# Stacking the bfloat16 parts of Q and K through DRAM instead of SBUF to SBUF, in a one-core decoder layer

## Chip, cores and metric

One core of one Trainium2 chip. The metric is the device time of one execution in microseconds. Engines: TensorE (PE, with PEld for its weight loads), VectorE (DVE), ScalarE (ACT), GpSimd (POOL) and SyncE (SP), which issues nearly all DMAs.

## What is computed

One pre-norm decoder layer on x of 4 x 256 x 256 (float32):

```
x = x + attn(layernorm(x))              # 16 heads of 16, rotary q and k, causal softmax, Wout
x = x + adjacency(ctx, layernorm(x))    # sim = Q K^T of ctx; keep the top 76 of 256 per row,
                                        # sigmoid, symmetrise: (1-g)*layernorm(x) + g*A
x = x + moe(layernorm(x))               # 64 experts of width 96, 6 of them per token,
                                        # grouped top-k routing, and a shared expert
```

## The kernel before, in words

The work has two phases. The attention phase goes over the four batches b = 0 to 3 (256 tokens each). Its steps run in one hand-written order for all engines, the list STEPS (line 73): every engine walks through the list and runs its own function for a step, if it has one (the `run` dictionaries, lines 686, 830, 987, 1387). The entries F4, F31 and so on in the list are VectorE's filler: so many instructions of the top-k search of the adjacency (maximum of 8 and match-replace, lines 1053 and 1058). The MoE phase follows: routing on VectorE, then 32 pairs of experts, with weights streamed through a ring of 16 slots and tokens gathered and scattered by GpSimd's indirect DMAs.

Q and K must keep float32 precision in the score product but go through TensorE as bfloat16. So each is split in three bfloat16 parts (part 0 the cast, part 1 the cast of the rest, part 2 what is left), and six of the products of parts are stacked along the contraction: for each head, Q's stack `qst` has 6 groups of 16 partitions that hold parts 0, 0, 0, 1, 1, 2 (TERMS_Q, line 59), K's stack `kst` has parts 0, 1, 2, 0, 1, 0. One matmul over 96 partitions then gives all six products.

The steps around the change, for one b:

- A2a (line 1127): VectorE reads the projected q and k out of PSUM, shuffles them and multiplies by the cosine; A2b adds the sine part (VectorE for b = 0, GpSimd after, lines 1143 and 930); ScalarE's `first_part` (757) casts to part 0.
- A2c, A2d: `first_rest` (VectorE 1150 or GpSimd 936), ScalarE's `second_part` (763), `third_part` (1155 or 941). GpSimd's third_part is followed by `gamma_constants` at b = 1 (902, its last instruction clears the tile `zero`) and by `moe_constants` at b = 2 (913).
- The parts stand in `parts` (184), one of two buffers by b % 2; the second buffer lies in slots 2 to 7 of `ring_dn`, the ring of expert down-weights. A part is 128 partitions of 1024 elements (Q has 2 x 256 of them, K the rest); partition p = 8 d + g holds dimension d of head pair g.
- SP's `stack` (359), in step A2d: for each part it waits until the part is there, then copies it with one DMA per place in the stacks, SBUF to SBUF. 12 DMAs of 128 KB for each b; a destination is 16 partitions of 8 KB. For b = 3 SP first waits for the last units of b = 0, whose stack it overwrites (373). After the stacks of b = 3 SP clears the scattered expert rows in DRAM with eight DMAs of 768 KB out of `zero` (380).
- U0 to U5 (521): TensorE computes six "S units" of scores of batch b (lines 478, 479) and six "T units" (490, 491) of batch b - 1. U0 waits for the whole stack of b (526). VectorE takes the maxima of each S unit (1176) and frees its bank, ScalarE exponentiates each T unit (784), GpSimd masks it (963), TensorE multiplies with the values (502, 506).
- V0 (`routing_constants`, 967): GpSimd fills constants of the MoE phase, among them the 32 unused partitions of `ring_dn` (973), a memset of 32 x 4096. It waits for the stacks of b = 3, since the second buffer of the parts lies there.
- D3a (1218, 1094): VectorE normalises the MoE's input, TensorE transposes it (577).

A wait on every DMA is by a semaphore that counts 16 for each. SP issues in order and waits in order.

Of the kernel before, what the change touches and what calls it, by code (L numbers as in the profile page):

```python
# [15 lines left out]
P = 128  # L16
# [18 lines left out]
RA = 8  # L35
# [79 lines left out]


def decoder_kernel(nc, x, cosT, sinT, ctxT, wxT, wqkvT, woT, gamma, gate_w, bias, w_gu, w_dn, ws_gu, ws_dn, out):
    x3_dram = nc.dram_tensor("moe_input", [T, E], F32, kind="Internal").ap()
    z_dram = nc.dram_tensor("expert_rows", [T * 8, E], F32, kind="Internal").ap()

    with ExitStack() as ctx:
# [40 lines left out]
        def cut(phase, *shape, dt=F32):  # L162
# [7 lines left out]
            if len(shape) > 1:  # L170
# [10 lines left out]
        xnT = cut(AT, 2, 2, S)  # L181
        qkc = cut(AT, 4, S)
        qks = cut(AT, 4, S)
        parts = [cut(AT, 3, 4, S, dt=BF16),
                 ring_dn[:, RA - 6:].rearrange("p r e n -> p (r e n)")[:, 0:6 * S].bitcast(BF16).rearrange("p (j a s) -> p j a s", j=3, a=4)]

        qst1, kst1 = cut(AT, H, S, dt=BF16), cut(AT, H, S, dt=BF16)
        simS = cut(AT, NT, S)
# [78 lines left out]

        x_in = [sem(f"x_in{b}") for b in range(B)]
        ctx_in, gamma_in, rope_in, wqkv_in, wo_in, moe_in = (sem(n) for n in ("ctx_in", "gamma_in", "rope_in", "wqkv_in", "wo_in", "moe_in"))
        stack_in = [sem(f"stack_in{b}") for b in range(B)]  # L270
        x3_out = sem("x3_out")
        z_zeroed = sem("z_zeroed")
# [65 lines left out]
        def _(sp):  # L338
# [17 lines left out]
                sp.dma_start(gate_up_weights(p).rearrange("p e c n -> p (e c n)"), w_gu[p]).then_inc(ring_in[p % RP], 16)  # L356
                sp.dma_start(down_weights(p)[0:FF].rearrange("p e n -> p (e n)"), w_dn[p]).then_inc(ring_in[p % RP], 16)

            def stack(b, j):

                sp.wait_ge((part0, part1, part2)[j], b + 1)
                for a, dst, terms in ((0, qst, TERMS_Q), (1, kst, TERMS_K)):
                    src = parts[b % 2][:, j, 2 * a:2 * a + 2, :].rearrange("p c s -> p (c s)")
                    for n, term in enumerate(terms):
                        if term == j:
                            to = dst[b % 3][n * D:(n + 1) * D].rearrange("p (g c) s -> p g (c s)", c=2)
                            sp.dma_start(to, src).then_inc(stack_in[b], 16)

            later = {("A2d", 1): range(0, 1), ("A2d", 2): range(1, RA - 6), ("D3a", 1): range(RA - 6, RA), ("D3a", 3): range(RA, RP)}
            for stage, b in STEPS:  # L370
                if stage == "A2d":
                    if b >= 3:
                        filled(sp, "unit", (T_UNITS[-1], b - 3))
                    for j in range(3):
                        stack(b, j)
                    if b == B - 1:
                        sp.wait_ge(zero_ready, 1)
                        zv = z_dram.rearrange("(t p k) n -> t p k n", p=P, k=8)
                        for t in range(NT):
                            sp.dma_start(zv[t, :, 0:KE, :], zero[:, :].unsqueeze(1).broadcast_to((P, KE, E))).then_inc(z_zeroed, 16)  # L380
                if stage == "D3a":
                    sp.wait_ge(x3_ready, b + 1)
                    sp.dma_start(x3_dram.rearrange("(t p) e -> p t e", p=P)[:, TPB * b:TPB * b + TPB, :],
                                 x3[:, TPB * b:TPB * b + TPB, :]).then_inc(x3_out, 16)
                if (stage, b) == ("D3a", 1):
                    filled(sp, "unit", (T_UNITS[-1], 2))
                if (stage, b) == ("D3a", B - 1):
                    filled(sp, "gen", ("att", B - 1))
                for p in later.get((stage, b), ()):
                    ring_fill(p)  # L390
# [24 lines left out]
        def _(pe):  # L415
# [105 lines left out]
            def units(n):  # L521
                def step(b):
                    if n == 0 and b >= 1:
                        emptied(pe, "gen", ("mT", b - 1))
                    if n == 0 and b < B:
                        pe.wait_ge(stack_in[b], 16 * 2 * len(TERMS_Q))
                    if b >= 1:
                        t_unit(b - 1, T_UNITS[n])
                    if b < B:
                        s_unit(b, S_UNITS[n])  # L530
                    if b >= 1 and n >= 3:
                        pv(b - 1, n - 3)
                return step
# [188 lines left out]
        def _(sc):  # L722
# [33 lines left out]

            def first_part(b):
                sc.wait_ge(roped, b + 1)
                if b >= 2:
                    sc.wait_ge(stack_in[b - 2], 16 * 2 * len(TERMS_Q))  # L760
                nc.scalar.copy(parts[b % 2][:, 0], qkc).then_inc(part0, 1)

            def second_part(b):
                sc.wait_ge(rest_ready, b + 1)
                nc.scalar.copy(parts[b % 2][:, 1], qkc).then_inc(part1, 1)

            def head_outputs(b, half):
                filled(sc, "out", (half, b))
# [90 lines left out]
        def _(gp):  # L859
# [53 lines left out]
            def moe_constants():  # L913

                link(pool.memset(tri[:, :], 1.0))
                link(pool.affine_select(out=tri[:, :], in_=tri[:, :], compare_op=ALU.is_ge, fill=0.0, base=-1,
                                        pattern=[[1, P]], channel_multiplier=-1))
                link(pool.memset(ones[:, :], 1.0))
                link(pool.iota(iotac[:, :, :], pattern=[[1, CAP], [0, NT]], base=-CP, channel_multiplier=0, allow_small_or_imprecise_dtypes=True))
                link(pool.memset(keep[:, :, :], 1.0))  # L920
                pool.memset(keep[:, :, 0:1], 0.0).then_inc(order_ready, 1)
                gp.wait_ge(order_ready, 1)

            def times_sin(b):
# [11 lines left out]
            def first_rest(b):  # L936
                if b >= 1:
                    gp.wait_ge(part0, b + 1)
                    pool.tensor_tensor(qkc, qkc, parts[b % 2][:, 0], ALU.subtract).then_inc(rest_ready, 1)

            def third_part(b):
                if b >= 1:
                    gp.wait_ge(part1, b + 1)
                    pool.tensor_tensor(parts[b % 2][:, 2], qkc, parts[b % 2][:, 1], ALU.subtract).then_inc(part2, 1)
                if b == 1:
                    gamma_constants()
                if b == 2:
                    moe_constants()
# [18 lines left out]
            def routing_constants(_):  # L967

                filled(gp, "gen", ("v", B - 1))
                gp.wait_ge(stack_in[B - 1], 16 * 2 * len(TERMS_Q))  # L970
                filled(gp, "unit", (T_UNITS[-1], 1))
                link(pool.memset(gsum, NEG))
                link(pool.memset(ring_dn[FF:P].rearrange("p a e n -> p (a e n)"), 0.0))
                link(pool.memset(gpick, NEG))
                link(pool.memset(epick, 3 * NEG))
                link(pool.memset(cand[:, :, NE:], 3 * NEG))
# [47 lines left out]
        def _(ve):  # L1024
# [125 lines left out]
            def first_rest(b):  # L1150
                if b == 0:
                    ve.wait_ge(part0, 1)
                    v.tensor_tensor(qkc, qkc, parts[b % 2][:, 0], ALU.subtract).then_inc(rest_ready, 1)

            def third_part(b):
                if b == 0:
                    ve.wait_ge(part1, 1)
                    v.tensor_tensor(parts[b % 2][:, 2], qkc, parts[b % 2][:, 1], ALU.subtract).then_inc(part2, 1)

            def shifts_turned(b):  # L1160
                if b >= 1:
# [59 lines left out]
            def routing(n):  # L1221
# [3 lines left out]
                ts = slice(t0, t1)  # L1225
                gs = slice(t0 * NG, t1 * NG)
                if n == 0:
                    ve.wait_ge(stack_in[B - 1], 16 * 2 * len(TERMS_Q))
                    filled(ve, "gen", ("v", B - 1))
                    ve.wait_ge(pick_ready, 1)  # L1230
                ve.wait_ge(score_ready, n + 1)
# [273 lines left out]
```

## Time and profile before

| | |
|---|---|
| median of 3 runs | 388.62 us (387.64 to 391.87) |
| profiled execution, its own time | 388.62 us |
| its span in the trace | 386.8 us |
| mean granted TensorE clock | 0.754 |
| busy: PE, PEld, DVE, ACT, POOL | 265.6, 192.3, 249.5, 90.3, 156.3 us |
| chain that ended last | PE 40%, DVE 25%, issue 8%, POOL 4%, DMA 2%, ACT 1% |
| stack DMAs | 48 of 128 KB |

The profiled execution's own time is the median itself; 1.8 us of it lie outside the span. The page gives busy times of each engine and the span in 40 slices of 9.67 us; the trace answers by line, by time (timeline), by stretch (windows) and by the chain of waits.

### The profile page before, as it was taken

To read this page: it belongs to the slowest core of one execution; us is meant where nothing else is said; L and a number is where in the kernel's file an instruction comes from. 1 tells how busy PE (TensorE), PEld (TensorE's weight loads), DVE (VectorE), ACT (ScalarE), POOL (GpSimd) and SP (SyncE) were. 2 spreads that over 40 slices of the span, in tenths; PEclk is the share of its full clock that TensorE was granted. 3 is DMA by queue.
4 is the path that set the end of the run, shared out by engine and by line. 5 is a ranking of instruction groups with operands and counts; after the bars stand their busy time and mean duration, and the time that the engine had idled before them with its cause. 6 is when DMAs were issued, how large, how long until landed. Compare 5 with 4: busy or idle time off the path is not lost.

```text
span 386.8 us, 6223 instructions
## 1 busy us (share of the span) xinstructions
PE 265.6 (69%) x2293; PEld 192.3 (50%) x2293; DVE 249.5 (64%) x655; ACT 90.3 (23%) x166; POOL 156.3 (40%) x160
## 2 busy tenths in 40 slices
PE   4681673686887895884915979998987979694000
PEld 1461653573674783653404468766656665362000
DVE  3769999996597558967699973241513403242897
ACT  2056001424332232441403000021211212241000
POOL 3727804848114123248833034225626244554000
PEclk9897767597997598797665776567857667999555
DMA  6349940950899300850009902146748460102982
GB/s 194 121 67 120 124 78 9 127 91 2 101 227 386 132 2 1 248 148 27 0 14 271 233 15 68 39 140 177 230 141 234 133 182 31 51 33 73 359 275 79
DMA packets 32141, 48.18 MB, mean 125 GB/s; under 512 B 4644, under 2 KB 22534, under 8 KB 32112
## 3 DMA queue, kind: packets, MB, share of 16 engines
q1 hardware_dynamic: 29424, 42.90, 45.2%
q0 software_dynamic: 2688, 4.89, 4.6%
q8 instruction: 18, 0.29, 0.3%
q14 instruction: 11, 0.09, 0.1%
HBM read 31.36 MB, written 12.58 MB: 114 GB/s over the span
## 4 chain that ended last, share of the span: by engine, by line
PE 40%; DVE 25%; issue 8%; POOL 4%; DMA 2%; ACT 1%; another core or an unknown queue 0%; POOLq 0%; DVEq 0%; SPq 0%
PE unit L667 8%; PE gen L644 7%; DVE arena L1453 6%; PE proj L682 4%; PE gen L635 3%; PE gen L569 2%; PE outp L675 2%; DVE arena L1058 2%; PE unit L490 2%; PE unit L653 2%; PE unit L491 2%; PE unit L478 2%; DVE arena L1176 1%; POOL expert_rows L1010 1%; PE unit L595 1%
## 5 line engine op out<-in xcount | busy, mean ns | idle before, releaser
L1010 POOL DMA_INDIRECT expert_rows<-arena x32 | 32.0, 1002 | 50.5 <-ACT arena L853 44.5
L1435 DVE TENSOR_TENSOR arena<-arena,unit 128x96 f32<-128x96 f32 x32 | 8.1, 252 | 60.9 <-ACT arena L846 57.0
L1005 POOL DMA_INDIRECT arena<-moe_input,arena x24 | 27.2, 1133 | 37.8 <-DVE arena L1372 31.4
L1176 DVE TENSOR_REDUCE arena<-unit 128x4 f32<-128x1024 f32 (+1 forms) x24 | 29.0, 1214 | 13.9 <-PE unit L479 13.9
L644 PE MATMUL gen<-arena 128*48 128x8 bf16 x512 | 28.2, 231 | 10.8 <-issue 10.1
L963 POOL TENSOR_SCALAR_AFFINE_SELECT arena<-arena 128x512 f32<-128x512 f32 (+1 forms) x24 | 19.2, 804 | 40.6 <-ACT arena L784 40.6
L784 ACT ACTIVATE arena<-unit 128x1024 f32<-128x1024 f32 x24 | 24.6, 1024 | 37.2 <-PE unit L491 37.2
L644 PEld LDWEIGHTS gen<-arena 128*48 128x48 bf16 x512 | 26.6, 184 | 11.9 <-issue 10.9
L1053 DVE MAX8 arena<-arena 128x8 f32<-128x256 f32 x80 | 29.9, 413 | 0.6 <-ACT arena L741 0.4
L1058 DVE MATCH_REPLACE8 arena<-arena 128x256 f32<-128x256 f32 x72 | 28.9, 408 | 0.0
L491 PE MATMUL unit<-arena 128*128 128x256 bf16 (+1 forms) x128 | 28.5, 281 | 0.0
L478 PE MATMUL unit<-arena 96*128 96x128 bf16 (+1 forms) x96 | 20.0, 292 | 8.8 <-DMA arena<-arena 7.9
L1453 DVE TENSOR_REDUCE arena<-arena 128x256 f32<-128x1536 f32 (+1 forms) x9 | 22.0, 2446 | 4.4 <-DMA arena<-expert_rows 4.4
L479 PE MATMUL unit<-arena,identb 128*128 128x128 bf16 x128 | 24.6, 253 | 0.0
L490 PE MATMUL unit<-arena 96*128 96x128 bf16 (+1 forms) x96 | 21.2, 279 | 3.9 <-ACT arena L784 3.9
L667 PE MATMUL unit<-ring,arena 128*64 128x192 f32 x128 | 18.8, 428 | 0.0
L880 POOL TENSOR_SCALAR srs<-mv 128x2 f32<-128x2 f32 x12 | 3.6, 299 | 36.2 <-DVE mv L1087 36.2
L853 ACT ACTIVATE arena<-proj,arena 128x256 f32<-128x256 f32 x32 | 15.2, 474 | 12.8 <-PE proj L682 10.2
L667 PE MATMUL unit<-arena 128*64 128x192 f32 x128 | 17.6, 407 | 0.5 <-issue 0.5
L460 PE MATMUL proj<-arena 128*128 128x256 f32 x64 | 16.6, 417 | 1.4 <-ACT arena L747 1.4
L478 PEld LDWEIGHTS unit<-arena 96*128 96x128 bf16 x96 | 11.6, 121 | 11.0 <-issue 8.2
L846 ACT ACTIVATE arena<-unit 128x96 f32<-128x96 f32 x32 | 8.0, 251 | 37.6 <-PE unit L667 37.6
(191 smaller groups left out, 616.2 us busy)
## 6 DMA issues: line engine op xcount, KB each, us to landing
ring<-in_w_gu SPq DMA_DIRECT2D x16, 384.0 KB, 6.6
expert_rows<-zero SPq DMA_DIRECT2D x8, 768.0 KB, 10.0
arena<-in_w_gu SPq DMA_DIRECT2D x16, 384.0 KB, 3.4
arena<-expert_rows SPq DMA_DIRECT2D x7, 768.0 KB, 5.8
arena<-ring_dn SPq DMA_DIRECT2D x24, 128.0 KB, 7.0
ring_dn<-in_w_dn SPq DMA_DIRECT2D x16, 192.0 KB, 6.9
arena<-in_w_dn SPq DMA_DIRECT2D x16, 192.0 KB, 4.0
arena<-arena SPq DMA_DIRECT2D x12, 128.0 KB, 5.9
```

Source lines behind the costliest of these rows:

```text
L478: mm(area, qst[b % 3][0:KT, h, t * P:(t + 1) * P], kst[b % 3][0:KT, h, 0:n], start=True, stop=False)
L479: last = mm(area[:, n - P:n], identb[:, :], masks, start=False, stop=True)
L490: mm(area, kst[b % 3][0:KT, h, kt * P:(kt + 1) * P], qst[b % 3][0:KT, h, kt * P:S], start=True, stop=False)
L491: last = mm(area, sel[:, h, :], nmT[:, kt * P:S], start=False, stop=True)
L644: last = mm(gen[CP * e:CP * e + CAP, q * 8:(q + 1) * 8], hotbuf[:, g % 2, 2 * q + e, :, t], vals[:, t, EPG * g + 2 * q + e, :], start=(t = ...
L667: last = mm(unit[CP * e:CP * e + CP, 1, (p % 2) * 512:(p % 2) * 512 + 2 * FF], xgT[:, g % 2, c, first:first + CP], gate_up_weights(p)[:, e ...
L1005: pool.indirect_dma_start(out=xg[:, k % NX, :], out_offset=None, in_=x3_dram, in_offset=bass.IndirectOffsetOnAxis(ap=toki[:, k:k + 1], axi ...
L1010: pool.indirect_dma_start(out=z_dram, out_offset=bass.IndirectOffsetOnAxis(ap=rowi[:, p:p + 1], axis=0), in_=yrow[:, p % NY, :], in_offset ...
L1053: last[i] = mark(v.max(best[:, i, :], simS[:, t + i, :] if r == 0 else work[:, i, :]))
L1058: last[i] = mark(v.match_replace(work[:, i, :], best[:, i, :], simS[:, t + i, :] if r == 0 else work[:, i, :], NEG))
L1176: v.tensor_reduce(nmax[:, t, c * u:c * u + c], unit_at((key, b)).rearrange("p (h k) -> p h k", k=n), axis=AX, op=ALU.max, negate=True).the ...
L1453: link(v.reduce_sum(fin[:, i % NZ, cols], zin[:, i % NZ, :, cols].rearrange("p k e -> p e k"), axis=AX))
```

## The change

The parts go through a new DRAM tensor `qk_dram`. For each b SP stores each part with one DMA of 256 KB (`store`), and loads the stacks from there with six DMAs (`load`): runs of neighbouring groups of 16 partitions go as one DMA where their parts are the same (Q's 0, 0, 0 and 1, 1: the source is repeated by a stride of zero) or follow each other (K's 0, 1, 2 and 0, 1). SP waits for each store before the loads that read it. There is one buffer of parts now: ScalarE's first_part of b waits for the three stores of b - 1. The clearing of the expert rows moves from behind the stacks of b = 3 to behind those of b = 1. The memset of ring_dn moves from GpSimd's routing_constants to the end of its moe_constants. Waits on the stacks of b = 3 that protected the parts become waits on its stores.

```diff
--- before.py
+++ after.py
@@ -115,6 +115,7 @@
 
 
 def decoder_kernel(nc, x, cosT, sinT, ctxT, wxT, wqkvT, woT, gamma, gate_w, bias, w_gu, w_dn, ws_gu, ws_dn, out):
+    qk_dram = nc.dram_tensor("qk_parts", [B, 2, 3, P, TPB * S], BF16, kind="Internal").ap()
     x3_dram = nc.dram_tensor("moe_input", [T, E], F32, kind="Internal").ap()
     z_dram = nc.dram_tensor("expert_rows", [T * 8, E], F32, kind="Internal").ap()
 
@@ -181,8 +182,7 @@
         xnT = cut(AT, 2, 2, S)
         qkc = cut(AT, 4, S)
         qks = cut(AT, 4, S)
-        parts = [cut(AT, 3, 4, S, dt=BF16),
-                 ring_dn[:, RA - 6:].rearrange("p r e n -> p (r e n)")[:, 0:6 * S].bitcast(BF16).rearrange("p (j a s) -> p j a s", j=3, a=4)]
+        parts = cut(AT, 3, 4, S, dt=BF16)
 
         qst1, kst1 = cut(AT, H, S, dt=BF16), cut(AT, H, S, dt=BF16)
         simS = cut(AT, NT, S)
@@ -267,6 +267,7 @@
 
         x_in = [sem(f"x_in{b}") for b in range(B)]
         ctx_in, gamma_in, rope_in, wqkv_in, wo_in, moe_in = (sem(n) for n in ("ctx_in", "gamma_in", "rope_in", "wqkv_in", "wo_in", "moe_in"))
+        parts_out = [[sem(f"parts_out{b}_{j}") for j in range(3)] for b in range(B)]
         stack_in = [sem(f"stack_in{b}") for b in range(B)]
         x3_out = sem("x3_out")
         z_zeroed = sem("z_zeroed")
@@ -356,24 +357,39 @@
                 sp.dma_start(gate_up_weights(p).rearrange("p e c n -> p (e c n)"), w_gu[p]).then_inc(ring_in[p % RP], 16)
                 sp.dma_start(down_weights(p)[0:FF].rearrange("p e n -> p (e n)"), w_dn[p]).then_inc(ring_in[p % RP], 16)
 
-            def stack(b, j):
+            def store(b, j):
 
                 sp.wait_ge((part0, part1, part2)[j], b + 1)
+                sp.dma_start(qk_dram[b, :, j].rearrange("a p n -> p a n"), parts[:, j].rearrange("p (a c) s -> p a (c s)", a=2)).then_inc(parts_out[b][j], 16)
+
+            def load(b, newest):
+
+
+                sp.wait_ge(parts_out[b][newest], 16)
                 for a, dst, terms in ((0, qst, TERMS_Q), (1, kst, TERMS_K)):
-                    src = parts[b % 2][:, j, 2 * a:2 * a + 2, :].rearrange("p c s -> p (c s)")
-                    for n, term in enumerate(terms):
-                        if term == j:
-                            to = dst[b % 3][n * D:(n + 1) * D].rearrange("p (g c) s -> p g (c s)", c=2)
-                            sp.dma_start(to, src).then_inc(stack_in[b], 16)
+                    for n, m in ((0, 3), (3, 2), (5, 1)):
+                        if max(terms[n:n + m]) != newest:
+                            continue
+                        to = dst[b % 3][n * D:(n + m) * D].rearrange("p h s -> p (h s)")
+                        src = qk_dram[b, a].rearrange("j (d h) n -> (j d) (h n)", d=D)
+                        if m > 1 and terms[n] == terms[n + 1]:
+                            src = src[terms[n] * D:(terms[n] + 1) * D].unsqueeze(0).broadcast_to((m, D, H * S))
+                        else:
+                            src = src[terms[n] * D:(terms[n] + m) * D]
+                        sp.dma_start(to, src).then_inc(stack_in[b], 16)
 
             later = {("A2d", 1): range(0, 1), ("A2d", 2): range(1, RA - 6), ("D3a", 1): range(RA - 6, RA), ("D3a", 3): range(RA, RP)}
             for stage, b in STEPS:
                 if stage == "A2d":
                     if b >= 3:
                         filled(sp, "unit", (T_UNITS[-1], b - 3))
-                    for j in range(3):
-                        stack(b, j)
-                    if b == B - 1:
+                    store(b, 0)
+                    store(b, 1)
+                    load(b, 0)
+                    store(b, 2)
+                    load(b, 1)
+                    load(b, 2)
+                    if b == 1:
                         sp.wait_ge(zero_ready, 1)
                         zv = z_dram.rearrange("(t p k) n -> t p k n", p=P, k=8)
                         for t in range(NT):
@@ -523,7 +539,7 @@
                     if n == 0 and b >= 1:
                         emptied(pe, "gen", ("mT", b - 1))
                     if n == 0 and b < B:
-                        pe.wait_ge(stack_in[b], 16 * 2 * len(TERMS_Q))
+                        pe.wait_ge(stack_in[b], 16 * 6)
                     if b >= 1:
                         t_unit(b - 1, T_UNITS[n])
                     if b < B:
@@ -756,13 +772,14 @@
 
             def first_part(b):
                 sc.wait_ge(roped, b + 1)
-                if b >= 2:
-                    sc.wait_ge(stack_in[b - 2], 16 * 2 * len(TERMS_Q))
-                nc.scalar.copy(parts[b % 2][:, 0], qkc).then_inc(part0, 1)
+                if b >= 1:
+                    for j in range(3):
+                        sc.wait_ge(parts_out[b - 1][j], 16)
+                nc.scalar.copy(parts[:, 0], qkc).then_inc(part0, 1)
 
             def second_part(b):
                 sc.wait_ge(rest_ready, b + 1)
-                nc.scalar.copy(parts[b % 2][:, 1], qkc).then_inc(part1, 1)
+                nc.scalar.copy(parts[:, 1], qkc).then_inc(part1, 1)
 
             def head_outputs(b, half):
                 filled(sc, "out", (half, b))
@@ -918,7 +935,8 @@
                 link(pool.memset(ones[:, :], 1.0))
                 link(pool.iota(iotac[:, :, :], pattern=[[1, CAP], [0, NT]], base=-CP, channel_multiplier=0, allow_small_or_imprecise_dtypes=True))
                 link(pool.memset(keep[:, :, :], 1.0))
-                pool.memset(keep[:, :, 0:1], 0.0).then_inc(order_ready, 1)
+                link(pool.memset(keep[:, :, 0:1], 0.0))
+                pool.memset(ring_dn[FF:P].rearrange("p a e n -> p (a e n)"), 0.0).then_inc(order_ready, 1)
                 gp.wait_ge(order_ready, 1)
 
             def times_sin(b):
@@ -936,12 +954,12 @@
             def first_rest(b):
                 if b >= 1:
                     gp.wait_ge(part0, b + 1)
-                    pool.tensor_tensor(qkc, qkc, parts[b % 2][:, 0], ALU.subtract).then_inc(rest_ready, 1)
+                    pool.tensor_tensor(qkc, qkc, parts[:, 0], ALU.subtract).then_inc(rest_ready, 1)
 
             def third_part(b):
                 if b >= 1:
                     gp.wait_ge(part1, b + 1)
-                    pool.tensor_tensor(parts[b % 2][:, 2], qkc, parts[b % 2][:, 1], ALU.subtract).then_inc(part2, 1)
+                    pool.tensor_tensor(parts[:, 2], qkc, parts[:, 1], ALU.subtract).then_inc(part2, 1)
                 if b == 1:
                     gamma_constants()
                 if b == 2:
@@ -967,10 +985,10 @@
             def routing_constants(_):
 
                 filled(gp, "gen", ("v", B - 1))
-                gp.wait_ge(stack_in[B - 1], 16 * 2 * len(TERMS_Q))
+                for j in range(3):
+                    gp.wait_ge(parts_out[B - 1][j], 16)
                 filled(gp, "unit", (T_UNITS[-1], 1))
                 link(pool.memset(gsum, NEG))
-                link(pool.memset(ring_dn[FF:P].rearrange("p a e n -> p (a e n)"), 0.0))
                 link(pool.memset(gpick, NEG))
                 link(pool.memset(epick, 3 * NEG))
                 link(pool.memset(cand[:, :, NE:], 3 * NEG))
@@ -1150,12 +1168,12 @@
             def first_rest(b):
                 if b == 0:
                     ve.wait_ge(part0, 1)
-                    v.tensor_tensor(qkc, qkc, parts[b % 2][:, 0], ALU.subtract).then_inc(rest_ready, 1)
+                    v.tensor_tensor(qkc, qkc, parts[:, 0], ALU.subtract).then_inc(rest_ready, 1)
 
             def third_part(b):
                 if b == 0:
                     ve.wait_ge(part1, 1)
-                    v.tensor_tensor(parts[b % 2][:, 2], qkc, parts[b % 2][:, 1], ALU.subtract).then_inc(part2, 1)
+                    v.tensor_tensor(parts[:, 2], qkc, parts[:, 1], ALU.subtract).then_inc(part2, 1)
 
             def shifts_turned(b):
                 if b >= 1:
@@ -1225,7 +1243,8 @@
                 ts = slice(t0, t1)
                 gs = slice(t0 * NG, t1 * NG)
                 if n == 0:
-                    ve.wait_ge(stack_in[B - 1], 16 * 2 * len(TERMS_Q))
+                    for j in range(3):
+                        ve.wait_ge(parts_out[B - 1][j], 16)
                     filled(ve, "gen", ("v", B - 1))
                     ve.wait_ge(pick_ready, 1)
                 ve.wait_ge(score_ready, n + 1)
```

## Rows read from the trace of the kernel before

**Rows 1.** The page, busy tenths of VectorE in 40 slices.

```profile
DVE  3769999996597558967699973241513403242897
```

**Rows 2.** The chain that ended last, first 135 us: start, us, what.

```profile
75.03 0.74 DVE arena L1053 x2
...
82.69 1.29 DVE arena L1133
...
89.35 1.04 ACT ring_dn L761
...
101.92 0.16 PE unit L490
```

**Rows 3.** Timeline of all engines, 18 to 72 us: start, us, engine, line.

```profile
24.37 1.04 ACT L765 CAST arena<-arena 128x1024 bf16<-128x1024 f32 x1 [0.80 <-DVE arena L1153]
...
25.45 1.23 DVE L1158 TENSOR_TENSOR arena<-arena 128x1024 bf16<-128x1024 f32 x1 [1.11 <-ACT arena L765]
...
33.60 1.04 ACT L761 CAST ring_dn<-arena 128x1024 bf16<-128x1024 f32 x1 [0.73 <-POOL arena L934]
...
38.65 0.27 PE L478 MATMUL unit<-arena 96*128 96x128 bf16 x1 [7.85 <-DMA arena<-arena]
...
42.01 2.55 PE L467 MATMUL gen<-arena 128*128 128x256 f32 x8
...
42.73 2.34 DVE L1176 TENSOR_REDUCE arena<-unit 128x8 f32<-128x1024 f32 x2
```

**Rows 4.** Timeline of VectorE: the normalisation of the MoE input, b = 2 and b = 3.

```profile
176.50 4.12 DVE L1094 TENSOR_SCALAR x<-res,mv,rstd 128x256 f32<-128x256 f32 x2 [0.57 <-POOL rstd L881]
...
201.03 0.73 DVE L1094 TENSOR_SCALAR x<-res,mv,rstd 128x256 f32<-128x256 f32 x2 [0.51 <-POOL rstd L881]
```

**Rows 5.** The chain that ended last, 165 to 232 us.

```profile
176.54 3.69 issue
...
180.77 1.10 PE gen L577 x4
```

**Rows 6.** Timeline of GpSimd.

```profile
78.67 0.64 POOL L963 TENSOR_SCALAR_AFFINE_SELECT arena<-arena 128x512 f32<-128x512 f32 x1 [0.93 <-ACT arena L784]
84.05 2.35 POOL L928 TENSOR_TENSOR arena<-arena 128x1024 f32<-128x1024 f32 x1 [4.75 <-DVE arena L1133]
...
176.65 3.51 POOL L973 MEMSET ring_dn<- 32x4096 f32 x1
...
181.47 3.52 POOL L979 MEMSET arena<- 128x4096 bf16 x1
```

**Rows 7.** Timeline of TensorE: its first product with the values.

```profile
87.04 0.64 PE L502 MATMUL outp<-arena 128*32 128x256 f32 x8
```

**Rows 8.** Timeline of SP's DMA issues.

```profile
23.10 7.76 SPq L367 DMA_DIRECT2D arena<-arena  x12
...
66.07 9.57 SPq L367 DMA_DIRECT2D ring<-arena  x12
...
105.55 16.78 SPq L380 DMA_DIRECT2D expert_rows<-zero  x8
```

**Rows 9.** Windows: us; busy of PE, PEld, DVE, ACT, POOL; clock; DMA share; GB/s.

```profile
5.00:7.00 2.00, 2.00 (x3) 0.80 (x3) 0.97 (x4) 0.00 (x0) 0.34 (x2) 1.00 1.00 391
...
212.00:214.00 2.00, 2.00 (x7) 1.55 (x6) 1.93 (x3) 1.13 (x1) 0.00 (x0) 0.50 1.07 270
...
30.00:35.00 5.00, 0.79 (x4) 0.36 (x2) 4.85 (x20) 3.92 (x5) 3.77 (x3) 0.80 1.14 123
...
118.00:123.00 5.00, 2.48 (x31) 1.63 (x30) 4.21 (x9) 1.95 (x3) 1.91 (x5) 0.87 1.09 386
```

**Rows 10.** The page, DMA issues: count, KB each, median us from issue to landing.

```profile
arena<-in_w_gu SPq DMA_DIRECT2D x16, 384.0 KB, 3.4
...
moe_input<-x SPq DMA_DIRECT2D x4, 256.0 KB, 2.2
```

## The prediction

> **What bounds the kernel now.** I read the page's slices first, then the chain of waits, then the timeline around each place that the diff touches. In the slices VectorE is busy for nine tenths and more from the fourth to the ninth, 29 to 87 us [rows 1]: this is the stretch in which the stacks of b = 0, 1 and 2 are made. The chain is followed back from the end only as far as 75 us, and there it stands on VectorE's filler, goes over the rotary step of b = 3 to ScalarE's cast of its part 0, and from 91 us on mostly over TensorE [rows 2]. Ahead of 75 us I take VectorE as the bound, since it has work without a gap from 30 us. So a thing that comes earlier between 30 and 83 us gains nothing unless VectorE waits for it, and a thing that makes VectorE wait costs in full.
>
> The one visible stall on the stacks is TensorE's: it starts the first score unit at 38.65 us after 7.85 us of waiting for the DMA [rows 3]. It looks like the target of such a change, but VectorE does not feel it. Its maxima of the first two units are taken at 42.73 us, in one run of 2.34 us, straight behind filler. The two units take TensorE from 38.65 to 42.01 us, 1.68 us each, so the first is complete at about 40.5 and the second at 42.2.
>
> A second stall is smaller in the page than on the chain: the normalisation of the MoE input of b = 2 takes 4.12 us for two instructions, where the same pair takes 0.73 us for b = 3 [rows 4]. The chain shows 3.69 us of it as "issue" and TensorE's transpose straight behind [rows 5]. What stands beside it is GpSimd's memset of ring_dn, 176.65 to 180.16 us [rows 6]: VectorE moves again when it ends.
>
> **The memset that moves.** It leaves the place where it blocks the chain. What is late next there are GpSimd's four short memsets (1.3 us, from 180.16 to 181.47) and then another of 3.52 us, which stands at 181.47 us and will follow at about 177.9 [rows 6]. VectorE's pair, started at 176.50, should be through by 177.3 to 177.6, between them. Gain: 4.12 - 0.73 = 3.4 at most, less up to 0.6 for the short ones; I take **3.1 us**. The bounds are 3.4, and 0 where the next long memset catches the pair. The rest of the chain follows it (transpose, router, shared expert, the next residual), and GpSimd's own constants come 3.5 us earlier too, so nothing there becomes late.
>
> At its new place, behind moe_constants at 76.5 us, the same 3.51 us are put ahead of two masks. The second ends at 79.3 now and would end at about 82.0; GpSimd then idles until 84.05 as before, for it had 4.75 us of idle [rows 6]. The first product with the values, which needs these masks, starts only at 87.04 us [rows 7]. VectorE's work in those microseconds is filler and a maximum out of PSUM, and it shows the same durations beside GpSimd's work earlier. Cost 0, with 2 us of cover; 2 us at most without it.
>
> **The stacks of b = 0.** Before, SP issues the 12 DMAs from 23.10 us and the stack has landed at 38.65: 15.55 us for 1.57 MB [rows 3, 8]. While they run the engines carry 123 GB/s, with every one of them busy, and the clearing of the expert rows gets 386 [rows 9]. So the stack copies are slow by their shape. Now: part 0 is stored at 23.1 and landed at 25.3 (a store of 256 KB takes 2.2 us to land [rows 10]); part 1 is there at 25.41 and part 2 at 26.68 [rows 3]. SP is held by part 1 before it issues the first loads, so these leave at about 26.1, 3.0 us later than the first copies did. The bytes loaded are the same 1.57 MB into the same partitions. By the nearest row, the copies of before, they take the same 15.55 us, and the store of part 2 among them 0.7 us (262 KB at 386). That is 26.1 + 15.55 + 0.7 = 42.3 us for the landed stack, 3.7 later than now. The store of part 2 and the last two loads are in series behind it, but in this reading the engines are full all the time, so the hops are hidden.
>
> From below: at the rates of plain loads, 270 to 391 GB/s [rows 9], part 2 would be landed at about 30.5, the last two loads issued by 31.7 and landed after 3.4 us more [rows 10], at about 35. From above: the two loads of Q whose source is repeated may not be spread evenly over the 16 engines (the second rival); that gives 47 us.
>
> What VectorE feels of a stack that lands at T: the second unit is complete at T + 3.6 and is wanted at 42.73 + 1.17 = 43.9, so the delay is T - 40.3 where positive. With T = 42.3 it is **2.0 us**, with 35 nothing, with 47 6.8. This delay goes to the end, because VectorE is full from there to the rotary step of b = 3 [rows 1, 2].
>
> A rule of the Trainium skill bears on the 123 GB/s. "SBUF — State Buffer", section "Door 1: The DMA port swizzle", says that a DMA's rate goes with how many of 16 ports its partitions reach, and 16 neighbouring partitions reach 4 of them; the page's 27 GB/s a port would give 109 here, near the 123 measured. By this rule loads of 32 or 48 partitions would run at twice the copies' rate, the stack would land near 37 us, and the term would be 0 instead of 2.0.
>
> **The stacks of b = 1 to 3, and the new waits.** ScalarE's first_part of b now waits for the stores of b - 1, with ScalarE's exponentials and copies queued behind it. For b = 1 the cast stands at 33.60 [rows 3] and the stores of b = 0 are in by 31 to 36: up to 2 us, which VectorE does not wait for. For b = 3 it stands on the chain at 89.35 [rows 2]. The stores of b = 2 come behind the clearing, which has moved. SP is done with b = 1 at about 53, then holds 16.8 us in the eight clearing DMAs [rows 8], so b = 2 starts at about 70 instead of 66.07, behind some 6 us of queued bytes. The store of part 2 lands at about 84, 5 us ahead of the cast, which by then is 2 us later too. The stack of b = 2 is wanted at 101.92 [rows 2] and lands near 90; b = 1 and b = 3 have more room. The clearing itself leaves 105 to 129 us, where nobody on the chain waits for a DMA. All this: 0, the bound above being the third place of the second rival.
>
> **The sum**, against the profiled execution's 388.6, which is also the median: 388.6 - 3.1 + 2.0 = **387.5 us**.
>
> **Rivals.** *First: the loads run well, and only the memset counts.* For it: plain loads reach 270 to 391 GB/s [rows 9]. Against it: they write the rows that took 123. The time is 388.6 - 3.1 = 385.5.
>
> *Second, slower than before: the repeated source puts two loads on few DMA engines.* The outermost dimension of the source is the 3 or the 2 repetitions. If a DMA is dealt out by that dimension, 128 KB of each of the two loads go through one engine, and all that is behind them in its queue waits, the store of part 2 first. One engine carries 391 / 16 = 24 GB/s at best and 270 / 16 = 17 in a stretch of weight loads [rows 9]: 5.4 to 7.7 us for 128 KB, twice, in series. T = 26.7 + twice that + 3.5 to 4.9 for the other shares of this engine and the landing = 41.0 to 47.0; VectorE's delay is 0.7 to 6.7 us. The midpoint, 3.7, with the memset's gain gives 389.2, the far end 392.2. It is slower than before where T is past 43.4. At the far end the store of part 2 of b = 2 also nears the cast at 89.35. For it: the copies show that the shape alone can cost a factor of three. Against it: no DMA of the trace has so small an outer dimension, so it can't be seen. The Trainium skill states it outright: "DMA: Bandwidth & Descriptors", section "Rules for kernel authors", says that a leading zero-stride broadcast of c copies confines the whole DMA to at most c engines; no row here shows it.
>
> *Third: the long memset behind catches the normalisation.* The gain of 3.1 goes, and with the stacks' 2.0 it is 390.6. Against it: VectorE got in between two memsets at 180.2 us, where the gap is equally short [rows 5, 6].
>
> *That the stall of 7.85 us was worth something* I give no case of its own: it would need VectorE to be idle ahead of 42.73, and it is not.
>
> **How the numbers follow.** 387.5: 0.38. First rival 0.27, second 0.22, third 0.08, others 0.05. The likeliest one's own range is 386 to 389. One per cent, 3.9 us, is about what can be told from no change here. Faster by over that, below 384.7, needs the first rival and another microsecond of gain, for which small shifts between VectorE and GpSimd are enough: 0.18. Slower than 392.5 needs the second at its far end with a wait of ScalarE on top: 0.12. Between them 0.70. The range of 8 in 10 is 384.4 to 392.0.
>
> **What would show it.** In the changed profile the normalisation of b = 2 takes under 1.3 us and no "issue" of over 1 us stands before the transpose; the memset stands at about 77 us (plus the delay) with GpSimd still idle behind it. TensorE's first score unit starts at 41 to 44 us, and VectorE shows a wait of some 2 us in front of the first maxima. A start at 35 and no wait says the first rival; the repeated loads landing 3 us or more after their neighbours say the second. A wait of ScalarE at line 761 of b = 3 would make the prediction wrong from the other side, as would a normalisation that is still at 4 us.

## The result, and the profile after

The changed kernel takes 390.48 us (median of 20, 386.97 to 394.32) where the kernel before takes 386.06 beside it (20, 383.43 to 392.27): a ratio of 1.0099, 95% interval 1.0069 to 1.0129, which is 3.8 us slower. Ratios in this document are taken over fast executions, those that did not run slow as a whole, so the medians of all executions differ by a little more, 4.4 us. The forecast was 1.1 us faster. Each profile is of one execution, and from about 226 us on the changed one ran without TensorE's "issue" gaps that the others have: 0.3 us idle ahead of the experts' products (L660) against 10.8 before. Its span is 367.2 us; the same kernel's next profile, the run again below, has 382.8. So profiles are compared below by stage, never by their ends.

First the page of the changed kernel, where its chain stood by engine and by line:

```profile
PE 44%; DVE 22%; DMA 15%; SPq 7%; issue 5%; POOL 3%; ACT 3%; POOLq 0%; ACTq 0%; DVEq 0%
DMA qk_parts<-arena 12%; PE unit L683 7%; PE gen L660 7%; DVE arena L1472 6%; SPq L396 4%; PE proj L698 4%; PE gen L651 3%; PE unit L611 2%; PE proj L639 2%; PE gen L585 2%; PE proj L449 2%; POOL expert_rows L1028 2%; PE outp L691 2%; PE unit L669 2%; DVE arena L1076 2%
```

The DMA had 2% of the chain before. Now it has 15%, 12% in stores of parts, and SP's own queue has 7%. The chain itself (start, us, what) says where, and it answers to [rows 2]:

```profile
26.21 0.86 SPq L379
27.55 11.01 DMA qk_parts<-arena
38.66 1.05 ACT arena L778
39.73 7.86 DMA qk_parts<-arena
47.60 0.72 SPq L379
48.84 9.64 DMA qk_parts<-arena
60.38 4.04 SPq L396
...
79.28 5.84 DMA qk_parts<-arena
85.14 0.71 SPq L379
86.38 10.58 DMA qk_parts<-arena
97.05 1.04 ACT arena L778
```

Read it as a sentence: a store of part 2 that lands after 11 us (a store of 256 KB took 2.2 us before [rows 10]) holds ScalarE's cast of b = 1; SP, held in the loads of b = 1, comes late to the clearing (L396), which holds the stores of b = 2; these hold the cast of b = 3. That cast stands at 97.05, 7.7 us behind the 89.35 of [rows 2]. Now SP's timeline, then TensorE's and VectorE's at the first score units, against [rows 3, 8]:

```profile
23.46 2.71 SPq L363 DMA_DIRECT2D qk_parts<-arena  x2
26.21 1.29 SPq L379 DMA_DIRECT2D arena<-qk_parts  x2
27.55 0.41 SPq L363 DMA_DIRECT2D qk_parts<-arena  x1
28.01 1.14 SPq L379 DMA_DIRECT2D arena<-qk_parts  x2
...
38.57 0.78 SPq L379 DMA_DIRECT2D arena<-qk_parts  x2
```

```profile
46.99 0.27 PE L494 MATMUL unit<-arena 96*128 96x128 bf16 x1 [15.84 <-DMA arena<-qk_parts]
...
48.89 1.22 DVE L1194 TENSOR_REDUCE arena<-unit 128x8 f32<-128x1024 f32 x1 [5.72 <-PE unit L495]
50.60 1.23 DVE L1194 TENSOR_REDUCE arena<-unit 128x8 f32<-128x1024 f32 x1 [0.48 <-PE unit L495]
```

SP issues four of the six loads by 29.2 us. The last two come 9.4 us later, since they need part 2 and its store, queued behind the first repeated load, lands only at 38.56. The stack of b = 0 lands at 47.0, and VectorE, which had no gap here before, waits 6.2 us. The windows say why (us; busy of five engines; clock; DMA share; GB/s):

```profile
32.00:34.00 2.00, 0.00 (x0) 0.00 (x0) 2.00 (x9) 1.23 (x2) 1.92 (x1) 0.88 0.20 61
34.00:36.00 2.00, 0.00 (x0) 0.00 (x0) 2.00 (x11) 0.00 (x0) 0.00 (x0) 0.50 0.20 61
36.00:38.00 2.00, 0.00 (x0) 0.00 (x0) 2.00 (x8) 0.00 (x0) 0.00 (x0) 0.50 0.18 60
...
45.00:46.00 1.00, 0.00 (x0) 0.00 (x0) 0.00 (x0) 0.00 (x0) 0.73 (x4) 0.50 0.07 29
46.00:47.00 1.00, 0.01 (x1) 0.04 (x2) 0.00 (x0) 0.00 (x0) 1.00 (x1) 0.50 0.06 22
```

A busy share of 0.18 to 0.20 is 3 of 16 engines, at 61 / 3 = 20 GB/s each; the copies of before kept all of them busy [rows 9]. If the load with three repetitions of 128 KB runs on three engines, it takes, by estimate, 131 KB / 20 GB/s = 6.5 us. In the last 2 us before the stack lands the share is 0.07 and 0.06, one engine of 16, which had more queued than the rest. The profile does not tell which load that engine carried. The Trainium skill's "DMA: Bandwidth & Descriptors", section "Rules for kernel authors", says that a source with a leading zero-stride dimension of c copies confines the DMA to at most c engines. The trace agrees for the load of three copies, with the share of 3 engines from 32 to 38 us; it does not show the load of two by itself.

ScalarE's timeline has the two casts that wait for a store, of b = 1 and b = 3:

```profile
38.66 1.05 ACT L778 CAST arena<-arena 128x1024 bf16<-128x1024 f32 x1 [5.42 <-DMA qk_parts<-arena]
...
97.05 1.04 ACT L778 CAST arena<-arena 128x1024 bf16<-128x1024 f32 x1 [5.69 <-DMA qk_parts<-arena]
```

Last the memset: GpSimd's timeline and VectorE's normalisation of b = 2, against [rows 4, 6]:

```profile
83.67 3.51 POOL L939 MEMSET ring_dn<- 32x4096 f32 x1
...
91.10 2.35 POOL L946 TENSOR_TENSOR arena<-arena 128x1024 f32<-128x1024 f32 x1 [2.17 <-DVE arena L1151]
...
181.49 3.51 POOL L997 MEMSET arena<- 128x4096 bf16 x1
```

```profile
180.09 0.76 DVE L1112 TENSOR_SCALAR x<-res,mv,rstd 128x256 f32<-128x256 f32 x2 [0.56 <-POOL rstd L898]
```

The pair takes 0.76 us instead of 4.12 and is done before the next long memset begins; at its new place the memset leaves GpSimd idle behind its masks, as forecast. The Trainium skill's "SBUF — State Buffer", section "Who interferes with whom", says that a VectorE instruction in a mode that uses both of its port pairs, which tensor_scalar can enter, shares one pair with GpSimd, and that the second to issue is blocked for the whole instruction of the first. The 4.12 us that end with a 3.51 us memset, and the 0.76 without it, agree; which mode the instruction ran in the trace does not show.

### The profile page after: what moved, and what is told of

It is laid out like the page before. It is cut to its first block, busy times and chain, and to the rows that moved or that the text cites. A ratio compares the mean times of both kernels' runs of the same rounds, so it can differ in the third digit from the quotient of the medians.

```text
span 367.2 us, 6217 instructions
## 1 busy us (share of the span) xinstructions
PE 253.0 (69%) x2293; PEld 184.1 (50%) x2293; DVE 244.7 (67%) x655; ACT 90.6 (25%) x166; POOL 155.7 (42%) x160
## 4 chain that ended last, share of the span: by engine, by line
PE 44%; DVE 22%; DMA 15%; SPq 7%; issue 5%; POOL 3%; ACT 3%; POOLq 0%; ACTq 0%; DVEq 0%
DMA qk_parts<-arena 12%; PE unit L683 7%; PE gen L660 7%; DVE arena L1472 6%; SPq L396 4%; PE proj L698 4%; PE gen L651 3%; PE unit L611 2%; PE proj L639 2%; PE gen L585 2%; PE proj L449 2%; POOL expert_rows L1028 2%; PE outp L691 2%; PE unit L669 2%; DVE arena L1076 2%
## 5 line engine op out<-in xcount | busy, mean ns | idle before, releaser
L494 PE MATMUL unit<-arena 96*128 96x128 bf16 (+1 forms) x96 | 18.9, 281 | 17.4 <-DMA arena<-qk_parts 15.8
L507 PE MATMUL unit<-arena 128*128 128x256 bf16 (+1 forms) x128 | 27.1, 271 | 0.0
L660 PE MATMUL gen<-arena 128*48 128x8 bf16 x512 | 24.4, 232 | 0.3 <-ACT arena L838 0.3
L506 PE MATMUL unit<-arena 96*128 96x128 bf16 (+1 forms) x96 | 21.3, 280 | 4.6 <-ACT arena L801 4.6
L660 PEld LDWEIGHTS gen<-arena 128*48 128x48 bf16 x512 | 23.7, 186 | 0.4 <-ACT arena L838 0.3
L495 PE MATMUL unit<-arena,identb 128*128 128x128 bf16 x128 | 23.2, 243 | 0.0
L683 PE MATMUL unit<-arena 128*64 128x192 f32 x128 | 16.6, 388 | 0.0
```

Source lines behind the costliest of these rows:

```text
L494: mm(area, qst[b % 3][0:KT, h, t * P:(t + 1) * P], kst[b % 3][0:KT, h, 0:n], start=True, stop=False)
L495: last = mm(area[:, n - P:n], identb[:, :], masks, start=False, stop=True)
L507: last = mm(area, sel[:, h, :], nmT[:, kt * P:S], start=False, stop=True)
L660: last = mm(gen[CP * e:CP * e + CAP, q * 8:(q + 1) * 8], hotbuf[:, g % 2, 2 * q + e, :, t], vals[:, t, EPG * g + 2 * q + e, :], start=(t = ...
L683: last = mm(unit[CP * e:CP * e + CP, 1, (p % 2) * 512:(p % 2) * 512 + 2 * FF], xgT[:, g % 2, c, first:first + CP], gate_up_weights(p)[:, e ...
```

## Experiments

All were timed in turn with the kernel before, in three batches, each on one chip (a ratio is to the kernel before on the same chip): again, split, memset_back and clear_back; split_memset_back, split_clear_back, memset_only and two_buffers; the repeats and split_b0.

**again**: the changed kernel itself.

> The changed kernel once more, to have a second profile of it beside its time. Few-engines theory (each load of Q with a repeated source runs on as many DMA engines as there are repetitions, and what stands behind it in their queues is late): ratio to before 1.01; TensorE's first score unit at 47 us, VectorE waits about 6 us for it, ScalarE's cast of part 0 of b = 3 waits 5 to 6 us for a store. The MoE phase, 142 us in the first profile of the changed kernel against 160 before, has the same instructions in both; if the difference belongs to the execution and not to the change, it comes out elsewhere here.

389.35 us, ratio 1.0134 (1.0089 to 1.018). Slower again. In its profile the first unit starts at 46.22 us and the cast of b = 3 waits 7.72 us for a store, more than the 5 to 6 expected. The span is 382.8 us, so the short last phase of the first profile belonged to that execution.

**split**: the repeated loads as one DMA of 16 partitions for each repetition, so 9 loads for a b.

```diff
-src = src[...].unsqueeze(0).broadcast_to((m, D, H * S))
+for i in range(m):
+    sp.dma_start(to[i * D:(i + 1) * D], src[...]).then_inc(stack_in[b], 16)
...
-pe.wait_ge(stack_in[b], 16 * 6)
+pe.wait_ge(stack_in[b], 16 * 9)
```

> The changed kernel, with the repeated loads issued as one plain DMA of 16 partitions for each repetition (nine loads for each b instead of six, the same bytes). Few-engines theory: the first score unit starts at 35 to 39 us, VectorE's wait of 6 us and both long waits of ScalarE go, and what is left of the change is the memset's gain: ratio to before about 0.991. Slow-rows theory (the loads are slow because of the partitions they write, as the SBUF copies of before were): the first unit stays at 42 us or later and the ratio above 1.0. Two-hops theory (the way through DRAM is what costs): the store of part 2 still lands 8 us or more after its issue.

377.85 us, ratio 0.9813 (0.9766 to 0.9859): 0.032 or some 12 us below again, beside it on the same chip, and well under the kernel before. The 0.991 expected allowed only 3.4 us for the memset; the surplus is followed up below. Its rows: TensorE's first unit, ScalarE's cast of b = 3, and a window of the loads.

```profile
39.48 0.27 PE L495 MATMUL unit<-arena 96*128 96x128 bf16 x1 [8.54 <-DMA arena<-qk_parts]
```

```profile
89.46 1.04 ACT L779 CAST arena<-arena 128x1024 bf16<-128x1024 f32 x1 [5.03 <-POOL arena L953]
```

```profile
34.00:36.00 2.00, 0.00 (x0) 0.00 (x0) 2.00 (x9) 0.78 (x1) 1.15 (x1) 0.50 1.01 172
```

All engines busy, the stack at 39.5, no wait on a store: 89.46 is within 0.1 us of [rows 2]. Issuing each repetition as a DMA of its own takes away the whole of the slow path.

**memset_back** (of the changed kernel) and **split_memset_back** (of split): the memset of ring_dn in routing_constants again.

```diff
-pool.memset(ring_dn[FF:P]...).then_inc(order_ready, 1)
...
+link(pool.memset(ring_dn[FF:P]..., 0.0))
```

> The changed kernel, with the memset of ring_dn back in GpSimd's routing constants. If VectorE's normalisation of b = 2 is blocked by that memset: it takes 4.1 us again instead of 0.76, and the kernel is 3.4 us slower than the changed one: ratio to before 1.019. If the memset costs nothing there: ratio as the changed kernel, 1.010.

> The path through DRAM with one DMA for each repetition (9 loads for a b) and the memset of ring_dn in its old place on GpSimd: the path alone, without the memset's move. Theory A, the loads on few DMA engines were the whole fault of the change and the memset's move is worth its 3.4 us: split measured 0.981, so this stands at 0.990 to 0.993 and the normalisation of b = 2 takes about 4 us again; what is left under 1 belongs to the path itself or to the earlier clearing. Rival B, the memset's new place is what made split good beyond 3.4 us: this stands at 1.00.

> The kernel of split_memset_back once more, the path through DRAM with evenly spread loads alone. It measured 1.006 where the milestones of split up to 176 us say 1.000. Theory A, no cost of the path: 0.998 to 1.004. Rival B, a cost of its own: 1.006 or more again.

memset_back: 393.76 us, 1.0246 (1.0203 to 1.0288), 4.4 us above again and above the 1.019 expected. split_memset_back: 1.006 (1.0032 to 1.0089), outside both theories and nearer rival B, and repeated 1.0015 (0.9981 to 1.0049), within theory A of the repeat. The path through DRAM with evenly spread loads alone is thus worth nothing, or costs half a per cent; it is no gain. The first run taken alone would have looked like its rival's cost.

**memset_only**: the kernel before, with only the memset moved. The second buffer of parts goes from ring_dn to x3T, so that the memset may run early, and ScalarE's first copy into x3T waits for the stacks of b = 3.

```diff
-ring_dn[:, RA - 6:]...[:, 0:6 * S].bitcast(BF16)...
+x3T.rearrange("p c t -> p (c t)")[:, 0:6 * S].bitcast(BF16)...
```

> The kernel before, with its stack copies from SBUF to SBUF, and only the memset of ring_dn moved to the end of moe_constants; so that this is free of races the second buffer of parts lies in x3T, and ScalarE's first copy into x3T waits for the stacks of b = 3, long done. Theory A: the normalisation of b = 2 falls from 4.1 to 0.7 us and the time by 3.1 to 3.4 us, 0.991 to 0.992. Rival B, the 3.4 us are taken up by a later wait in the MoE phase: 1.00.

> The kernel of memset_only once more (copies from SBUF to SBUF, the memset of ring_dn moved). Theory A: 0.983 to 0.989, the 3.4 us of the blocked normalisation and about 2 us more, since TensorE does not idle ahead of the shared expert's products of b = 3 and keeps its clock there. Rival B, only the 3.4 us: 0.991.

0.9874 (0.9834 to 0.9914), repeated 0.9848 (0.9795 to 0.9901): 4.9 and 5.9 us gained, more than the 3.4 of the blocked pair and than the 0.991 first expected. **split2**, beside the second, measured 0.9826 (0.9779 to 0.9873):

> The kernel of split once more, to see whether its 0.981 repeats on the chip on which memset_only is timed beside it. In split's profile every milestone up to 176 us stands within 0.2 us of before's (cast of b = 3 at 89.46 against 89.35, first copy of the MoE input at 127.72 against 127.63), so theory A says that the path through DRAM is worth nothing with evenly spread loads, and the memset's move all: split2 and memset_only2 agree within 1%, both at 0.982 to 0.990. Rival B, the path itself is a gain: split2 stays at 0.981 and memset_only2 above 0.987.

The two agree within their intervals, as theory A had it, so no gain of the path is seen beside that of the memset. Where the surplus over 3.4 us lies is seen between ScalarE's copies of the MoE input of b = 1 and b = 3. This takes 46.1 to 46.6 us in all four profiles with the memset in its old place (before: 156.45 to 203.04), and 40.1 to 41.0 in nine of the ten without (split: 156.53 to 197.36; split_b0, below, has 42.5). Chain pieces of memset_back, then of clear_back (below), which differs by the memset and the clearing:

```profile
182.68 3.69 issue
...
188.72 1.95 PE gen L603 x8
...
192.13 5.50 PE unit L611 x8
```

```profile
185.94 1.09 PE gen L603 x8
...
188.48 4.42 PE unit L611 x8
```

Behind the stall of 3.69 us the router's and the shared expert's products take 1.9 us more. Windows of the 6 us from the first of these transposes, in the kernel before and in clear_back, have the granted clock (third number from the right):

```profile
180.77:186.77 6.00, 4.92 (x18) 3.79 (x19) 0.81 (x2) 2.72 (x5) 5.81 (x4) 0.50 0.13 44
```

```profile
184.59:190.59 6.00, 4.92 (x19) 3.11 (x20) 2.02 (x6) 4.02 (x6) 5.87 (x3) 0.72 0.13 44
```

It is 0.50, the lower of TensorE's two levels (1.2 GHz of 2.4), for all 6 us in each of the four profiles with the stall, and 0.63 to 1.00 in the ten without. The transposes take 1.09 us in the four and 0.63 in the ten. The stall is not the only thing that the lower clock follows: split_b0 has no stall there, 0.63, and products nearly as slow.

**clear_back** (of the changed kernel) and **split_clear_back** (of split): the clearing behind the stacks of b = 3 again (`if b == 1:` to `if b == B - 1:`).

> The changed kernel, with the clearing of the expert rows back behind the stacks of b = 3. If the clearing is what makes the stores of b = 2 late: ScalarE's cast of part 0 of b = 3 waits under 1 us instead of 5.7, and the kernel is some 5 us faster than the changed one, ratio to before 0.997. If the loads of Q alone make them late: the wait stays above 4 us and the ratio at 1.01. The 6 us at the first unit of b = 0 stay in either case.

> The split loads with the memset moved, and the clearing of the expert rows in its old place behind the stacks of b = 3. With the loads of the change that edit gained some 4 us, since the clearing held up the store of b = 2. Theory A, the earlier clearing costs only where the stores are late: with the split loads nothing is waited for, so putting it back changes nothing, 0.981. Rival B, the clearing taken out of 105 to 129 us is itself where split's surplus over the memset's 3.4 us comes from: 0.990 to 0.993.

clear_back: 1.0018 (0.9982 to 1.0055), 0.0116 or some 4 us below again, a little less than expected. split_clear_back: 0.9917 (0.9887 to 0.9947), not the 0.981 of theory A but within its rival B. Memset_only, which also clears late, has 0.9874 beside it and a gain over 3.4 us, so the surplus does not need the early clearing. Split was not timed on this chip, and whether early clearing is worth something with fast loads stays open. With slow loads it costs. The cast of b = 3 in clear_back:

```profile
96.64 1.04 ACT L778 CAST arena<-arena 128x1024 bf16<-128x1024 f32 x1 [5.04 <-POOL arena L952]
```

It waits for GpSimd's half of the rotary step again, not for a store. The profile shows 1.3 us of the 4 (the table below); the rest stays open.

**two_buffers**: the changed kernel with a second buffer of parts in x3T; first_part waits for the stores of b - 2.

```diff
-parts = cut(AT, 3, 4, S, dt=BF16)
+parts = [cut(AT, 3, 4, S, dt=BF16), x3T...[:, 0:6 * S].bitcast(BF16)...]
...
-if b >= 1: ... sc.wait_ge(parts_out[b - 1][j], 16)
+if b >= 2: ... sc.wait_ge(parts_out[b - 2][j], 16)
```

> The changed kernel with its slow loads, and two buffers of parts again (the second in x3T), so that ScalarE's first_part waits for the stores of b - 2 only. Theory A, two waits make the loss, VectorE's of 6 us at b = 0 and ScalarE's of 5 to 8 us ahead of the cast of b = 3: the second one goes, and the time falls by about 4 us from that of again, 1.0134, to 1.002 to 1.005. Rival B, ScalarE's wait is hidden behind VectorE's filler and the wait at b = 0 is all: 1.013. In both the first score unit of b = 0 still starts at about 47 us.

1.0108 (1.0069 to 1.0147): a miss for theory A. ScalarE waits for no store any more, but the time barely moves; by the timed runs rival B is nearer. The table below has 0.7 and 2.7 us for that wait, not 4. Yet clear_back, in which ScalarE's wait is gone too, measured 1.0018 on another chip, and nothing in the table accounts for the difference.

**split_b0**: split's loads for b = 0 only.

> The changed kernel with the repeated loads split for b = 0 only; b = 1 to 3 keep the loads with the repeated source. Theory A, the wait of VectorE on the first stack and that of ScalarE ahead of the cast of b = 1 are 5 to 7 of the 8 us that the slow loads cost: the first unit starts at 39.5 us, the cast of b = 1 has no wait, the cast of b = 3 has a wait on the stores of b = 2 of at most 3 us beyond its usual one, and the ratio is 0.985 to 0.995. Rival B, the stacks of b = 1 to 3 cost as much: 1.00 or more.

0.9924 (0.9887 to 0.9961), within theory A. The first unit starts at 38.49 us, the cast of b = 1 waits for no store, and that of b = 3 waits for a store:

```profile
93.26 1.04 ACT L782 CAST arena<-arena 128x1024 bf16<-128x1024 f32 x1 [6.09 <-DMA qk_parts<-arena]
```

## Why the prediction was wrong

The time moved the other way than forecast. The table takes the path of the slow loads out of the profiles. The stretch runs from VectorE's shuffle of b = 1 to the cast of b = 3, 61.96 us in the kernel before (27.39 to 89.35). The ScalarE column is what the step from the cast of b = 2 to that of b = 3 has beyond 24.36 us, its length wherever no store is waited for.

| profile | VectorE's wait at the first maxima | ScalarE, cast of b = 3 | stretch beyond 61.96 |
|---|---|---|---|
| split | 0 | 0 | 0.0 |
| changed | 6.2 | 0.7 | 7.4 |
| again | 5.6 | 2.7 | 8.3 |
| clear_back | 6.9 | 0 | 7.0 |
| two_buffers | 3.3 | 0 | 3.4 |
| split_b0 | 0 | 1.1 | 1.2 |

The two waits add up to the delay within half a microsecond. Two_buffers has less of the first for a reason of its own: its projection of b = 1 took 6.10 us instead of 3.72, so VectorE came 2.3 us later to the same late stack.

- **The step that failed: the stack of b = 0.** The prediction took "the nearest row, the copies of before" for all six loads and got T = 42.3 and 2.0 us. What happened was its second rival: T = 47.0, as its bound from above said, and 6.2 us of wait against 6.7. That the landing agrees to the tenth is partly luck. The rival had 15.4 us for two loads at 17 GB/s an engine and 4.9 behind them; an engine carried 20, which makes 13 us, and the last two loads, issued at 38.57 behind the store, landed 8.4 us later. The premise, a source with only 3 or 2 outer repetitions, was in the diff. The prediction counted against it that no DMA of the trace has that shape, but this only meant that the trace could not speak on it; "the nearest row" was of another shape.
- **The second step that failed: the waits of ScalarE at b = 3, costed at 0.** The store of part 2 of b = 2 was put at 84 us, landed. It landed at 96.96: SP, held in the slow loads of b = 0 and 1, came to the clearing at 59.33 us instead of 53 and to the stores of b = 2 at 79.28 instead of 70, and the store then took 10.6 us behind the slow loads of its own b. Cost 0.7 to 2.7 us. That the wait at b = 1 is not felt was right, though it was 5.4 us long and not 2: clear_back has it (5.85 us) and its delay is VectorE's wait alone.
- **The memset: right in mechanism, under-sized.** The pair gave 4.12 - 0.76 = 3.4 us, between two memsets as forecast; the third rival is refuted. But the stage as a whole gives 5.8 (46.6 in memset_back, 40.8 in clear_back), of which 0.5 are the transposes straight behind (1.10 against 0.64) and 1.9 the products. The term of 3.1 had no row for TensorE's clock behind the stall. The cover at the new place held.
- **The first rival**'s run of loads did not occur here. Split shows that it was within reach: with all engines busy the stack lands at 39.5, less than the 40.3 from which VectorE feels it, though not the 35 of that rival. At what rate loads of 32 or 48 partitions run by themselves no run shows; split's mix of loads has 139 to 172 GB/s between 32 and 38 us.

The sum: -5.8 for the memset and +7.4 to +8.3 for the waits is +1.6 to +2.5, and measured were +3.8 and, in again, +5.2. The missing 1 to 3 us lie outside these stretches, and the cause stays open. There the profiles fall in groups whatever the kernel. From the cast of b = 3 to the copy of the MoE input of b = 1 it is 62.4 to 63.5 us in eight of fourteen, with a granted clock of 0.89 to 0.92 in 90 to 135 us, and 67.0 to 67.1 in five, with 0.78 to 0.86. The projection of b = 1, ahead of the stretch, takes 3.72 us in nine and 6.09 to 6.39 in five, with a granted clock in 18 to 30 us of 0.92 to 1.00 and of 0.72. Whether a kernel's waits decide how often it gets which, and so explain the remainder and the miss of two_buffers, was not shown.

## What to carry to other kernels

Look at the outermost dimension of a DMA's source before its bytes: with three repetitions in front only three engines were busy here, and what stood behind it in SP's queue, wanted by another engine, paid too. When a profile shows two stalls, test each alone. TensorE's stall of 7.85 us, the visible one, had room behind it: in split the first unit starts 0.8 us later than before and nothing behind it moves (what removing the stall would be worth, no run tested). A memset of 3.5 us on an engine with room was worth 1.3 to 1.5% by itself. The best kernels of this study, split (0.981, 0.983) and memset_only (0.987, 0.985), have that move in common, and the path through DRAM adds no gain that these runs can tell. When all rows have another shape than the new code, they don't count against a rival.

## What was not expected of the hardware

- A DMA on few engines delays what is queued behind it on all others: a 256 KB store landed after 11.01 us instead of 2.2, and SP, whose next loads wait for that store, stood still for 9.4 us of it.
- A stall of TensorE can cost more than its length: 3.7 us ahead of the transposes of b = 2 came with the lower clock straight behind it in all four profiles that have the stall, and with 2.4 us of slower transposes and products in memset_back against clear_back.
- Executions of one kernel differ by as much as the change, and their granted clock with them: five executions of split at a mean granted clock of 0.782 or 0.783 took 376.02 to 378.17 us, two at about 0.76 took 382.47 and 385.26.
